# Attention scores inside a chunk: seven two-way levels with 14 matrix products become four passes of fours and pairs with 8

## The reference, cut to what matters

```python
b = jnp.cumsum(gt, axis=1)
diff = b[:, :, None, :] - b[:, None, :, :]
D = jnp.exp(jnp.where(mask, diff, -jnp.inf))
A = jnp.einsum('bik,bjk,bijk->bij', qt, kt, D)
o = o_inter + jnp.einsum('bij,bjv->biv', A, vt)
# and the other branch, from the same normalised x
h = jax.nn.silu(_tlin(x, w1_w, w1_s)) * _tlin(x, w2_w, w2_s)
h = jax.nn.gelu(_tlin(h, h1_w, h1_s), approximate=False)
h = jax.nn.gelu(_tlin(h, h2_w, h2_s), approximate=False)
return _tlin(h, w3_w, w3_s)
```

## Time and profile before

| what | us |
|---|---|
| median of three runs | 1967.26 (1966.08 to 1968.80) |
| the profiled execution | 1966.91 |
| its span | 1965.0 |
| TensorE busy | 1947.1 (99%) |
| VectorE busy | 1581.9 (81%) |
| ScalarE busy | 1266.0 (64%) |
| GpSimd busy | 68.4 (3%) |

### The profile page before, as it was taken

One profiled execution on the slowest core, in us unless ns is written; L12 is line 12 of the kernel. 1 busy time (PEld: TensorE's weight loads), 2 busy tenths in 40 slices (PEclk: granted clock), 3 DMA queues, 4 the chain that ended last, 5 costly groups with the idle time before them and its releaser, 6 DMA issues.

```text
span 1965.0 us, 46591 instructions
## 1 busy us (share of the span) xinstructions
PE 1947.1 (99%) x17348; PEld 1932.8 (98%) x17348; DVE 1581.9 (81%) x4274; ACT 1266.0 (64%) x2527; POOL 68.4 (3%) x104
## 2 busy tenths in 40 slices
PE   7999999999999999999999999999999999999998
PEld 7999999999999999999999999999999999999998
DVE  7787878878788887887878788787888878878777
ACT  5665656666566666666656566666666666666564
POOL 0000000000000000000000000000000000000000
PEclk9999999999999999999999999999999999999999
DMA  8000000000000000000000000000000000000000
GB/s 305 7 12 12 12 7 6 12 12 12 12 1 12 12 12 12 12 1 12 12 12 12 7 6 12 12 12 12 1 12 12 12 12 12 2 12 12 12 7 8
DMA packets 23360, 34.22 MB, mean 17 GB/s; under 512 B 2945, under 2 KB 19713, under 8 KB 23186
## 3 DMA queue, kind: packets, MB, share of 16 engines
q1 hardware_dynamic: 23186, 31.46, 4.8%
HBM read 23.07 MB, written 8.39 MB: 16 GB/s over the span
## 4 chain that ended last, share of the span: by engine, by line
PE 95%; issue 2%; DVE 1%; ACT 1%; SPq 1%; DMA 0%; POOLq 0%; POOL 0%; DVEq 0%; ACTq 0%
PE fb L364 64%; PE ab L364 22%; PE ab L568 2%; PE ab L601 1%; PE ab L509 1%; PE ab L498 1%; PE ab L434 1%; PE fb L649 1%; PE ab L561 0%; SPq L272 0%; PE ab L580 0%; DVE hid0l L944 0%; PE ab L560 0%; DMA small<-stage_w 0%; ACT raw L805 0%
## 5 line engine op out<-in xcount | busy, mean ns | idle before, releaser
L364 PE MATMUL fb<-hid1h,wwhole 128*128 128x256 f32 x2048 | 475.0, 280 | 1.1 <-DVE hid1l L861 1.1
L364 PE MATMUL fb<-hid1l,wwhole 128*128 128x256 f32 x2048 | 468.5, 277 | 0.0
L364 PE MATMUL fb<-hid0l,wwhole 128*128 128x256 f32 x2048 | 465.9, 276 | 0.0
L364 PE MATMUL fb<-hid0h,wwhole 128*128 128x256 f32 x2048 | 465.8, 276 | 0.0
L364 PEld LDWEIGHTS fb<-hid1h,wwhole 128*128 128x128 f32 x2048 | 384.7, 188 | 3.8 <-ACT hid1h L720 0.8
L364 PEld LDWEIGHTS fb<-hid1l,wwhole 128*128 128x128 f32 x2048 | 384.9, 188 | 0.0
L364 PEld LDWEIGHTS fb<-hid0l,wwhole 128*128 128x128 f32 x2048 | 384.6, 188 | 0.0
L364 PEld LDWEIGHTS fb<-hid0h,wwhole 128*128 128x128 f32 x2048 | 384.5, 188 | 0.0
L805 ACT ACTIVATE raw<-fb,sh_s 128x256 f32<-128x256 f32 x512 | 212.7, 467 | 127.0 <-PE fb L364 124.8
L364 PE MATMUL fb<-xntl,wwhole 128*128 128x256 f32 x1024 | 237.5, 277 | 0.0
L364 PE MATMUL fb<-xnth,wwhole 128*128 128x256 f32 x1024 | 237.5, 277 | 0.0
(11 more groups left out here) (217 smaller groups left out, 4514.0 us busy)
## 6 DMA issues: line engine op xcount, KB each, us to landing
xin<-x SPq DMA_DIRECT2D x32, 256.0 KB, 2.7
out<-xin SPq DMA_DIRECT2D x32, 256.0 KB, 2.6
stage_more<-stage_w SPq DMA_DIRECT2D x6, 512.0 KB, 7.3
sgate<-stage_w SPq DMA_DIRECT2D x4, 512.0 KB, 5.5
shift<-stage_w SPq DMA_DIRECT2D x4, 512.0 KB, 5.6
v<-stage_w SPq DMA_DIRECT2D x4, 512.0 KB, 5.8
raw<-stage_w SPq DMA_DIRECT2D x3, 512.0 KB, 6.1
mixed<-stage_w SPq DMA_DIRECT2D x3, 512.0 KB, 8.5
```

The source lines that it names most:

```text
L364: mm = pe.matmul(o, a, b, start=start and i == 0, stop=stop and i == len(pairs) - 1)
```

## The change

The scores' triangle is cut into four levels instead of seven: steps of 32 tokens (a chunk as four quarters), of 8, of 2, and single pairs of neighbours. In a level of fours a key is scaled once, and a later query once for each quarter between (`lev_q` has up to three copies, so 192 columns). The diagonal comes with the pair level. TensorE's products per half go from 14 with 64 columns to 8: two with 192 (pairs and diagonal), four with 192, two with 128. The two products with `pair_ones` go; the keys are squared on GpSimd (`k_sq`), transposed by TensorE and summed by VectorE. ScalarE's two squares go and six small exponentials for the widest level come; its large exponential has 704 columns instead of 896. VectorE's masking by rows becomes a chain of multiplications by block masks and additions, kept unscaled by `rkn`, which ScalarE and VectorE apply at the end. The state update now also waits for nine of the eleven merges, since their source is in the bank that it overwrites.

```diff
+STEP = (32, 8, 2)
...
-        kx, qs = bsum[rows(1), :], small[rows(0), 4:6, :]
+        kx, qs = t3[rows(1), :], small[rows(0), UP + 4 * CH:UP + 6 * CH].rearrange("p (c t) -> p c t", c=NC)
+        def later(ap, m, r):
+            return ap.rearrange("p (s t) -> p s t", t=4 * m)[:, :, (r + 1) * m:]
+        def streamed(ap, m, r):
+            first, n = (0, 3, 5)[r] * CH // 4, (3 - r) * CH // 4
+            return ap[..., first:first + n].rearrange("p (s t) -> p s t" if len(ap.shape) == 2 else "p c (s t) -> p c s t", t=(3 - r) * m)
...
+                pool.wait_ge(qk_ev.sem, qk_ev.at(me, 2 * NC))
+                pool.tensor_tensor(k_sq[:], k_s, k_s, ALU.mult).then_inc(ksq_d.sem, 1)
...
-                pe.matmul(ab[3][:, N:N + NC], t4, pair_ones[:], start=True, stop=True)
-                pe.matmul(ab[3][:, N + NC:N + 2 * NC], qk, pair_ones[:], start=True, stop=True)
+                pe.wait_ge(ksq_d.sem, ksq_d.at(me))
+                pe.transpose(ab[2][:, CH + MOVING:2 * CH + MOVING], k_sq[:], ident_s[:]).then_inc(sq_mm.sem, 1)
...
-                for i in range(LEVELS):
+                pe.wait_ge(far_d.sem, far_d.at(me))
+                for c in range(NC):
+                    pe.matmul(pair_out[:, c, :], kg[rows(c), :], pair_q[rows(c), :], start=True, stop=True)
+                for i in (2, 1, 0):
                     for c in range(NC):
-                        mm = pe.matmul(ab[c][:, i * UP:(i + 1) * UP], lev[rows(c), i, :], levq[rows(c), i, :], start=True, stop=True)
+                        mm = pe.matmul(lev_out[i][:, c, :], lev_k[i][rows(c), :], lev_q[i][rows(c), :], start=True, stop=True)
                 mm.then_inc(lv_mm.sem, 1)
...
+                    pe.wait_ge(att_d.sem, att_d.at(me, 9))
...
+                    pe.wait_ge(att_sc.sem, att_sc.at(me))
...
-                for c in range(NC):
-                    act.activation(t4[rows(c), :], ab[2][K:P, c * CH:(c + 1) * CH], ACT.Square).then_inc(qk_ev.sem, 1)
+                act.activation(lev_k[0][:, 0:64], bsum[:, 0:64], ACT.Exp, bias=nb[:, 1:2]).then_inc(far_d.sem, 1)
+                act.activation(lev_k[0][:, 64:96], bsum[:, 64:96], ACT.Exp, bias=nb[:, 2:3]).then_inc(far_d.sem, 1)
+                act.activation(lev_k[0][:, 96:CH], bsum[:, 0:32], ACT.Exp, bias=nb[:, 0:1]).then_inc(far_d.sem, 1)
+                act.activation(lev_q[0][:, 0:32], bsum[:, 32:64], ACT.Exp, bias=bsum[:, 31:32], scale=-1.0).then_inc(far_d.sem, 1)
+                act.activation(lev_q[0][:, 32:96], bsum[:, 64:CH], ACT.Exp, bias=bsum[:, 63:64], scale=-1.0).then_inc(far_d.sem, 1)
+                act.activation(lev_q[0][:, 96:CH], bsum[:, 96:CH], ACT.Exp, bias=bsum[:, 95:96], scale=-1.0).then_inc(far_d.sem, 1)
                 act.wait_ge(levarg_d.sem, levarg_d.at(me))
-                act.activation(lev[:], lev[:], ACT.Exp, scale=-1.0).then_inc(lev_d.sem, 1)
+                act.activation(near, near, ACT.Exp, scale=-1.0).then_inc(lev_d.sem, 1)
...
-                        act.activation(atth[:, 0, :], att[:, 0, :], ACT.Copy).then_inc(att_hi.sem, 1)
+                        act.activation(att[:, 1, :], att[:, 1, :], ACT.Copy, scale=rkn[:, 1:2]).then_inc(att_sc.sem, 1)
+                        act.activation(atth[:, 0, :], att[:, 0, :], ACT.Copy, scale=rkn[:, 0:1]).then_inc(att_hi.sem, 1)
...
+                for i in (1, 2):
+                    m = STEP[i]
+                    b, s = bsum.rearrange("p (g r) -> p g r", r=m), CH // (4 * m)
+                    dve.tensor_tensor(lev_k[i].rearrange("p (g r) -> p g r", r=m), b[:, :, m - 1:m].to_broadcast([P, CH // m, m]), b, ALU.subtract)
+                    for r in range(3):
+                        end = later(bsum, m, r - 1)[:, :, m - 1:m].to_broadcast([P, s, (3 - r) * m])
+                        dve.tensor_tensor(streamed(lev_q[i], m, r), later(bsum, m, r), end, ALU.subtract)
...
+                def fours(i, r):
+                    m = STEP[i]
+                    merge_before()
+                    upper = att[:].rearrange("p c (s t) -> p c s t", t=4 * m)[:, :, :, (r + 1) * m:]
+                    merge(dve.scalar_tensor_tensor(upper, streamed(lev_out[i], m, r), sub_block[2 - i][:, r:r + 1],
+                                                   upper, ALU.mult, ALU.add))
...
-                dve.wait_ge(dg_mm.sem, dg_mm.at(me))
-                dve.tensor_copy(qk_sum[:], ab[3][:, N + NC:N + 2 * NC])
-                dve.tensor_scalar(ssk[:], ab[3][:, N:N + NC], KEPS2, None, ALU.max).then_inc(ss_d.sem, 1)
+                dve.wait_ge(sq_mm.sem, sq_mm.at(me))
+                dve.wait_ge(lv_mm.sem, lv_mm.at(me))
+                dve.tensor_reduce(ssk[:], ab[2][:, CH + MOVING:2 * CH + MOVING].rearrange("p (c k) -> p c k", c=NC), mybir.AxisListType.X,
+                                  ALU.add).then_inc(sq_k.sem, 1)
+                dve.wait_ge(sq_k.sem, sq_k.at(me))
+                dve.tensor_scalar(ssk[:], ssk[:], KEPS2, None, ALU.max).then_inc(ss_d.sem, 1)
                 hidden_low(hid1l, hid1h, 2, hid1_hi, hid1_lo)
+                hidden_low(hid1l, hid1h, 3, hid1_hi, hid1_lo)
+                pairs()
+                for r in range(3):
+                    fours(2, r)
...
+                within(2)
+                for r in range(3):
+                    fours(1, r)
+                within(1)
+                thirty_twos()
```

More of the change, by code:

```diff
@@ L22 @@
 UP = CH // 2
+MOVING = 3 * CH // 2
+STEP = (32, 8, 2)
 EPS = 1e-5
@@ L231, in layer_program @@
         G_POLY = G_ABS + LOG_DEG + 2
-        q_s, k_s, bsum, t1, t2, t3, t4, t5 = (small[:, i, :] for i in range(8))
+        q_s, k_s, bsum, t1, t2, t3, t4, t5 = (small[:, UP + i * CH:UP + (i + 1) * CH] for i in range(8))
+        pair_q, kg = small[:, 0:UP + CH], t4
+        nbt = nb[:, 3:4]
         e2, odd = att[:, 0, :], att[:, 1, :]
-        qk = att[:, 0, :]
         vh, vl = (t[:].rearrange("p d t -> p (d t)").rearrange("p (c d) -> p c d", c=NC) for t in (parth, partl))
@@ new lines, in half @@
+                for i in (1, 2):
+                    for r in range(3):
+                        dve.tensor_tensor(streamed(lev_q[i], STEP[i], r), streamed(lev_q[i], STEP[i], r), later(q_s, STEP[i], r), ALU.mult)
+                dve.tensor_tensor(pair_q[:, 0:UP], lev_1, q_s.rearrange("p (u two) -> p u two", two=2)[:, :, 1], ALU.mult).then_inc(levq_d.sem, 1)
+                both = work[:, CH:3 * CH].rearrange("p (l t) -> p l t", l=2)
+                dve.tensor_tensor(both, both, kg.unsqueeze(1).to_broadcast([P, 2, CH]), ALU.mult).then_inc(levk_d.sem, 1)
```

135 lines of the change are left out of this document (75 added, 60 removed).

## The result

The changed kernel takes 1988.23 us (median of 4 runs, 1986.07 to 1988.52) where the kernel before took 1967.77 in the same rounds. The ratio is 1.0102, with a 95% interval of 1.0089 to 1.0114. The forecast was 1983.5, with a range of 1969 to 1997. The profiled execution took 1988.52, 21.6 more than the 1966.91 of before.

A forecast was written before the change was run, and what follows sets the result against it. TensorE at 99% was taken as the bound, a chain to hid1l close behind. Per half 0.27 later, 0.24 release and restart, 0.32 slower pace, less 0.28 or 0.34 slack: 16.4 in all, forecast 1983.5 us, range 1969 to 1997.

The forecast's parts named there:

- The bound: Behind TensorE at 99%, the chain gates, decays, exponentials, gelus, hid1l is only 0.28 or 0.34 us shorter per half.
- TensorE's saving: Fewer score products and one transposition for the pair_ones products: TensorE reaches h2 0.7 to 1.0 us earlier per half.
- ScalarE's stage: Six small exponentials (1.36 us) and a 704-column one replace squares and large exponential; table load and gelus 0.27 us later.
- The slack and the release: At h2's wait for hid1l: slack 0.28 or 0.34 us; waiting costs 0.15 for release and 0.09 for restart.
- The sign of waits: Profile after shows TensorE waiting about 1 us per half for hid1l, 25 to 40 us in all, against 1.1 before.
- GpSimd: Rival: squaring of keys holds VectorE's decay chain through shared SBUF ports, 0.25 us per half, 1991.5 us; chance 0.17.
- The slow pace: After a wait, h2's 72 products run at 117.7 ns instead of 113.3: 0.32 us in every half.
- The prologue: Before the first half: smaller mask table, four fills replaced by five VectorE reductions; put at 0.3 us.
- The late scores: Rival: att merges, forecast 1.8 us longer with 1 us left, delay outputs by 0.3 per half, about 1993; chance 0.07.
- Six exponentials without overlap: Bound for ScalarE's stage: without overlap the six small exponentials take 1.9 us, chain 0.9 us longer.
- the chances for slower: Probability of a measurable slowdown, beyond about 0.2% or 3.9 us, given as 0.79 after rounding.
- the sum of 16.4: Total added time: 0.55 and 0.49 us for sixteen halves each, less 0.5 for the disturbed half, plus 0.3 for prologue.

The follow-up runs named there:

- experiment 2: Kernel before, TensorE forming the score products of only five of seven levels (4 of 14 left out): 1970.52 us.
- experiment 10: On experiment 9, the third pair's hid1h copy made by VectorE instead of ScalarE, keys' norms steps behind the third hid1l: 1950.39 us, ratio 0.9911.
- experiment 11: Changed kernel with only the third hid1h copy made by VectorE, keys' norms behind the third hid1l: 1971.26 us.
- experiment 12: Kernel before with only the third hid1h copy made by VectorE, norms left in place: 1967.39 us.
- experiment 5: Kernel before plus one unneeded exponential of 64 columns on ScalarE behind the large one: 1970.44 us.
- experiment 1: Changed kernel, GpSimd squaring the keys only after VectorE has all its differences of decay sums: 1981.28 us.
- experiment 8: Changed kernel with delayed GpSimd squaring, six exponentials exchanged for two, and prologue mask reductions ahead of VectorE's wait for TensorE: 1961.19 us, ratio 0.9966.
- experiment 9: On experiment 8, large exponential in pieces: 256 columns of near keys, 448 of near queries, then the far level's 256 in one: 1959.54 us.
- experiment 3: Kernel before plus two unneeded instructions: a 128-column exponential with bias on ScalarE and a 128-column product on GpSimd: 1986.28 us.
- experiment 6: Changed kernel, six small exponentials exchanged for VectorE differences and two plain 128-column exponentials behind the large one: 1970.09 us.

## Why the prediction came out right, and where its numbers were off

**The bound** was read rightly: a second chain behind a TensorE at 99%, 0.28 and 0.34 us shorter. Experiments 2, 10, 11 and 12 show it from all sides: less for TensorE alone gives nothing (2), a shorter chain alone gives nothing (12), each with the other gives 17 us (10), and on the changed kernel a chain shorter by 0.52 gives 17 of its 21 us back (11).

**TensorE's saving**, given as 0.7 to 1.0, is 0.54. A pair of 192 columns steps by 0.16, the upper end of the prediction (0.168), not 0.112, and the transposition in place of the products with `pair_ones` saved 0.24 (0.44 from 202.05 to 202.49 before, 0.20 from 205.69 to 205.89 now), not 0.33. As it said, the size made no difference to the end.

**ScalarE's stage** was given as 0.27 later, and is: 2.98 - 2.72. The six exponentials, worked out as 1.36, take 1.34. Lengths of neighbours and their overlap were enough for that.

**The slack and the release**: the piece is ready 0.147 us before its product and the next step is 0.08 too long, as the one row of before had it. What the prediction added up as two costs is one late weight load (experiment 5).

**The sign of waits** was 25 to 40 us for `hid1l`. The view reads 14.7, under it; by the starts of the products it is 30.

**GpSimd**: this is the part that was mis-sized most. It was a rival with a chance of 0.17, at 0.25 per half; it came true beside the forecast, at 0.23 and 0.22, and experiment 1 took it out for 7 us. The argument against it was the overlap at 204.88, where `hid1l` kept its 0.69 beside GpSimd's instruction of two columns; the trace of after has that overlap in every half too, again with 0.69. So an instruction of two columns was no measure for one that reads 128. Why the small one lets VectorE pass, no run shows. The rule of the Trainium skill ("SBUF — State Buffer", "Who interferes with whom") has a VectorE instruction with two SBUF inputs and a GpSimd instruction that reads SBUF take turns by whole instructions. The halves with `p` = 1 agree: the product takes 0.50 and not 0.28, and ends 0.15 behind the squaring. With `p` = 0 it was the copy of 12 columns ahead of the product that was held, until the squaring's end.

**The slow pace** was given as 0.32 in every half. It is 0.30, but in 16 of 32 halves, 0.15 on the mean: the time from the resumed product to the 96th is either 8.14 or 8.44. In the half shown above the pace after the third piece is 118 ns and after the fourth 113.4, so each wait settles it anew. What decides between the two stays open; every kernel in which most halves wait shows both.

**The prologue** was given as 0.3 and cost 2.0 in the profiled execution. Between 51 and 54 us TensorE did 13 products at a granted clock of 0.50 (1.2 GHz of 2.4), where it did 28 at full clock before; 15 x 0.11 = 1.6 us is most of the 2.0. That isn't the change's own: the kernel before with one more exponential had it too (experiment 5), and the changed kernel with one more wait on GpSimd had not (experiment 1).

**The late scores** didn't happen: VectorE's last step on `attl` in the fourth half, and TensorE's first product with it (they answer to the earlier trace rows):

```profile
278.11 0.35 DVE L1209 SCALAR_TENSOR_TENSOR attl<-att,rkn,atth 128x128 fp32r<-128x128 f32 x1 [0.77 <-ACT atth L863]
```
```profile
279.86 0.28 PE L383 MATMUL ab<-atth,parth 128*128 128x256 f32 x1
```

The outputs start 1.4 us behind `attl`, where the prediction had left 1; before it was 3.1. The merges take 1.9 us more behind the fourth `hid1l` (7.3 and not 5.4), close to the 1.8 given; but the terms printed for the 1.8 add up to 1.55.

**Slips in the working.** Six exponentials without overlap would lengthen the chain by 0.8, not 0.9 (1.9 + 0.79 - 1.86), and the chances for slower add up to 0.81, not 0.79. The forecast hangs on neither.

So the sum of 16.4 fell short by 5 us, from terms that erred in both directions: 7.2 for GpSimd, 1.7 for the prologue and 1.8 for the rest of the halves were missing, while 32 x 0.17 = 5.4 too much stood there for the pace. The direction and the wait come from the mechanism; that the number is so near is in part luck, since errors of 10.7 and 5.4 stood against each other.

## What to carry to other kernels

Before taking work from an engine at 99%, look up by how much the next chain is shorter, in clock readings of the last handover; if that is less than the saving, shorten the chain in the same change, for instance by giving a copy to the engine that stands idle at the handover. A product must find its operand ready 0.23 us ahead here, early enough for its weight load (0.218 wasn't enough in experiment 5, 0.227 was), and a miss by a hair costs 0.1 to 0.4 us, not the hair. The view of waits lists such misses in part or not at all (no line in experiments 5, 8 and 9); the starts of weight loads and products show them. Anything new on GpSimd belongs where VectorE's critical instructions aren't.

## What the runs showed of the hardware

- Beside a GpSimd product of 128 columns (0.40 us) VectorE's copy of 12 columns takes 0.40 and not 0.17, and with `p` = 1 its product of two tiles 0.50 and not 0.28. A GpSimd power of two columns (0.69 us) that overlaps a VectorE subtraction of 512 columns by 0.2 to 0.5 us leaves it at its 0.69.
- A matrix product whose operand arrives late starts 0.147 us behind it, its weight load 0.116 behind it, and the next product 0.34 behind it. If the operand is ready 0.17 to 0.22 ahead, the next step is still 0.01 to 0.05 too long; ready 0.227 or 0.238 ahead, it is free.
- After such a wait TensorE goes on at 113.4 or at 117.7 ns for a product, at full granted clock both times, in changing proportion (11 slow ones of 32 in experiment 1, 22 in experiments 8 and 9, none in 14 waiting halves with `p` = 0 of experiment 5).
- A pair of float32 products with 192 columns steps by 0.16 us, one with 64 by about 0.11.
- A copy with rounding of 128x512 takes VectorE 0.43 us and ScalarE 0.63.
- TensorE's granted clock was at 0.50 to 0.60 between 51 and 54 us, behind a pause in the prologue, in six of the 14 profiled executions (after, experiments 3, 5, 6, 9 and 10) and at 1.00 in the other eight, among both the old prologues and the new.
